# The second expert layer of a two-layer kernel, turned so that its hidden features lie on the partitions

## What is computed

```python
# x: (1024, 256), 32 experts, INTER = 96, TOP_K = 8, TAU = 0.05
logits = x @ gate_weight.T
probs = softmax(logits)
topv, topi = top_k(probs, TOP_K)
# ... thresholded by TAU and renormalised: routing_weights
combine = zeros((T, 32)).at[arange(T)[:, None], topi].add(routing_weights)

def expert_step(acc, xs):
    w_gu, w_d, c_e = xs
    gu = x @ w_gu.T
    g, u = split(gu, 2, axis=-1)
    h = silu(g) * u
    return acc + h @ w_d.T * c_e[:, None], None
out = scan(expert_step, zeros_like(x), (gate_up_proj, down_proj, combine.T))
x = _layernorm(x + out)
```

## Time and profile before

| | us |
|---|---|
| median of 3 runs | 672.63 |
| the three runs | 671.83, 672.63, 681.43 |
| span of the profiled execution (first to last instruction) | 627.6 |
| PE busy in it | 555.8 (89%) |
| DVE, ACT, POOL busy | 354.2, 237.4, 269.0 |
| mean granted clock of PE | 0.945 |

### The profile page before, as it was taken

The page is one execution under the profiler, slowest core; times in us unless marked ns, Lnnn a source line. Parts: engine busy times, 40 slices in busy tenths (PEclk is TensorE's granted clock), DMA queues, the critical chain, the costliest instruction groups (busy, mean ns, idle before and its releaser), DMA issues.

```text
span 627.6 us, 11175 instructions
## 1 busy us (share of the span) xinstructions
PE 555.8 (89%) x3453; PEld 481.3 (77%) x3453; DVE 354.2 (56%) x970; ACT 237.4 (38%) x617; POOL 269.0 (43%) x257
## 2 busy tenths in 40 slices
PE   8999985099989999989887778899999999999994
PEld 4666675078879889866444566899999999999994
DVE  4636686636664444338999566664444443444445
ACT  4645542245546665336020142233332333323234
POOL 3484024778987877602787600004042240404000
PEclk9979997589999999989998797899999999999998
DMA  8999891255876676400000420002020202000001
GB/s 259 372 387 384 284 333 52 105 177 168 232 225 188 192 237 185 133 0 1 1 1 0 152 75 2 0 1 70 8 77 2 76 0 75 0 0 0 0 0 67
DMA packets 58605, 70.93 MB, mean 113 GB/s; under 512 B 5681, under 2 KB 53570, under 8 KB 58562
## 3 DMA queue, kind: packets, MB, share of 16 engines
q10 hardware_dynamic: 35968, 35.26, 16.9%
q1 hardware_dynamic: 19234, 26.18, 13.4%
q0 software_dynamic: 3360, 8.93, 4.5%
...
## 4 chain that ended last, share of the span: by engine, by line
PE 67%; DVE 11%; DMA 5%; issue 4%; POOL 3%; ACT 3%; ACTq 1%; DVEq 0%; POOLq 0%
PE PS L1746 47%; DMA FA<-xg 5%; PE PS L2040 3%; POOL xg L662 3%; DVE FA L1700 2%; PE PS L1970 2%; DVE PS L1682 2%; PE PS L2065 2%; PE PS L2176 1%; PE PS L1821 1%; PE PS L1843 1%; PE PS L2089 1%; PE PS L2188 1%; PE PS L1983 1%; PE PS L1806 1%
## 5 line engine op out<-in xcount | busy, mean ns | idle before, releaser
L1746 PE MATMUL PS<-EW,XH 128*128 128x384 f32 (+3 forms) x764 | 215.4, 364 | 6.7 <-DVE SQ L1485 3.1
L1746 PEld LDWEIGHTS PS<-EW,XH 128*128 128x128 f32 x764 | 131.4, 193 | 11.9 <-DVE SQ L1485 3.4
L1485 DVE SCALAR_TENSOR_TENSOR SQ<-SIL,CW,PS 128x96 f32<-128x96 f32 x256 | 69.0, 311 | 116.6 <-ACT SIL L918 115.8
L1746 PE MATMUL PS<-EW,XL 128*128 128x384 f32 (+3 forms) x382 | 133.6, 350 | 0.0
L1746 PE MATMUL PS<-EW,EHH 128*128 128x256 f32 (+1 forms) x476 | 102.3, 290 | 0.2
L918 ACT ACTIVATE SIL<-PS 128x192 f32<-128x192 f32 x128 | 42.6, 332 | 158.0 <-PE PS L1746 158.0
L1746 PE MATMUL PS<-EW,EHL 128*128 128x256 f32 (+1 forms) x286 | 80.4, 281 | 0.0
L1746 PEld LDWEIGHTS PS<-EW,EHH 128*128 128x128 f32 (+1 forms) x476 | 78.5, 189 | 1.4 <-issue 0.6
L629 POOL TENSOR_TENSOR round_mark<-round_mark 128x1 f32<-128x1 f32 x10 | 1.9, 194 | 175.0 <-PE PS L1746 167.9
L1746 PEld LDWEIGHTS PS<-EW,XL 128*128 128x128 f32 x382 | 73.2, 192 | 2.1
L1746 PEld LDWEIGHTS PS<-EW,EHL 128*128 128x128 f32 (+1 forms) x286 | 54.0, 189 | 0.0
(11 more groups left out here) (373 smaller groups left out, 1048.5 us busy)
## 6 DMA issues: line engine op xcount, KB each, us to landing
...
FA<-xg ACTq DMA_DIRECT2D x47, 128.0 KB, 2.9
yg<-FA ACTq DMA_DIRECT2D x47, 128.0 KB, 3.0
...
EG<-in_gateup SPq DMA_DIRECT2D x4, 768.0 KB, 4.5
FA<-in_gateup SPq DMA_DIRECT2D x4, 768.0 KB, 4.6
```

Source lines behind the costliest of these rows:

```text
L1485: ins = dve.scalar_tensor_tensor(out=HH[:, pos % 2, h:h + W], in0=SIL[:, s, j * W:(j + 1) * W], scalar=c, in1=bank(s)[:, I + j * W:I + (j ...
L1746: ins = pe.matmul(o, l, r, start=start and i == 0, stop=stop and i == n - 1, skip_group_check=True)
```

## The change

The order of the second expert layer is turned. The gate/up weights become the stationary operand, 128 hidden features (a chunk; three chunks make a quad's 384) at a time, and 512 tokens (a half) move; so the hidden features come out on the partitions, in which form `down` takes them as its stationary operand, and no transposes are needed. There are 8 quads x 3 chunks x 2 halves = 48 steps, halves inside. A step has 12 matmuls of 512 columns (6 for gate, 6 for up, in two banks) and, 10 steps later (`LAG`), 12 of 256 columns (4 token tiles x 3).

With the features on the partitions the routing weight is no longer a scalar per partition but a row over tokens, the same for the 96 partitions of an expert. `CW` is made whole on DVE ahead of the steps, PE turns it (`turn_weights`, behind step 5), ACT and DVE copy it out, SP stores it to DRAM (`cw_room`, 128 KB) and reads it back spread over the partitions: for each pair of steps 512 KB in two DMAs (`load_spread`; one read serves both halves), in two buffers. POOL multiplies with it (`weighted`). The product silu x up is made by POOL in the first six steps (`AHEAD`, up copied by ACT) and by DVE from step 6.

The gate/up weights are loaded in four DMAs a quad, and POOL splits the quads 2 to 7 piece by piece between its steps (`next_split`). The residual moves ahead of the router. The router's products now have 128 tokens stationary and 64 columns moving (32 matmuls) and come out with tokens on the partitions; DVE adds the two halves. The last layer norm works in two halves of 4 tiles, the first waiting for all steps but the last. In place of a loop all steps are written out. Four semaphores of the first layer become one, with no change of order.

```diff
+        CHUNKS = 3
+        QUADS = E1 // QUAD
+        STEPS = QUADS * 2 * CHUNKS
+        LAG = 10
+        AHEAD = 6
+        MIXED, SPREADS, TURNED = 13, 2, 3
+        mixed = FA[:, KD * QUAD * 2 * I1:KD * QUAD * 2 * I1 + MIXED * BANK].rearrange("p (s c) -> p s c", s=MIXED)
...
+        def step_of(i):
+            return i // (2 * CHUNKS), i % 2, i // 2 % CHUNKS
+        def step_bank(i):
+            return 2 * ((i + 1) % 2 if i < AHEAD else i % 2)
+        def bank_before(i):
+            return i - 1 if i == AHEAD else i - 2
...
+            def load_spread(i):
+                n = i // 2
+                q, _, c = step_of(i)
+                if n >= SPREADS:
+                    sp.wait_ge(weighted, 2 * (n - SPREADS + 1))
...
+            sp.wait_ge(cw_step, CW_COPIED)
+            sp.dma_start(cw_room, cw_turned).then_inc(cw_stored, 16)
+            sp.wait_ge(cw_stored, 16)
+            for i in range(STEPS):
+                if i % 2 == 0:
+                    load_spread(i)
+                q = i // 6 + 4
+                if i % 6 == 2 and q < QUADS:
+                    load_gate(q)
+                q = (i - 11) // 6 + 4
+                if i >= 11 and i % 6 == 5 and q < QUADS:
+                    load_down(q)
...
+            def next_split(i):
+                at, j = divmod(i, 2 * CHUNKS)
+                q = at + 1
+                if 2 <= q < QUADS:
+                    g, gh, gl, _, _, _ = quad_slot(q)
+                    if j == 0:
+                        pool.wait_ge(gate_up_mm, 2 * 2 * CHUNKS * (q - 1))
+                        pool.wait_ge(gate_ld[q % 2], 32 * KD * (q // 2 + 1))
+                        rounded["g0"] = high(gh, g, half(0))
+                    if j == 2:
+                        low(gl, g, gh, half(0), rounded["g0"])
+                    if j == 3:
+                        rounded["g1"] = high(gh, g, half(1))
+                    if j == 4:
+                        low(gl, g, gh, half(1), rounded["g1"]).then_inc(gate_split, 1)
+                q = at - 1
+                if 2 <= q < QUADS:
+                    _, _, _, d, dh, dl = quad_slot(q)
+                    if j == 0:
+                        pool.wait_ge(dn_done, 2 * CHUNKS * (q - 1))
+                        pool.wait_ge(down_ld[q % 2], 16 * (q // 2 + 1))
+                        rounded["d"] = high(dh, d, whole)
+                    if j == 1:
+                        low(dl, d, dh, whole, rounded["d"]).then_inc(down_split, 1)
+            rounded = {}
+            for i in range(STEPS + LAG - 1):
+                if i < AHEAD:
+                    pool.wait_ge(sil_done, i + 1)
+                    pool.wait_ge(up_copied, i + 1)
+                    pool.tensor_tensor(mixed[:, i % MIXED, :], sil_t[:, i % 2, :], up_t[:, i % 2, :], ALU.mult
+                                       ).then_inc(mixed_pool, 1)
+                v = i - (LAG - 1)
+                if v >= 0:
+                    if v < AHEAD:
+                        pool.wait_ge(mixed_pool, v + 1)
+                    else:
+                        pool.wait_ge(mixed_dve, v - AHEAD + 1)
+                    n = v // 2
+                    pool.wait_ge(spread_ld[n % SPREADS], 32 * (n // SPREADS + 1))
+                    pool.tensor_tensor(mixed[:, v % MIXED, :], mixed[:, v % MIXED, :],
+                                       spread_w[n % SPREADS][:, v % 2 * BANK:(v % 2 + 1) * BANK], ALU.mult
+                                       ).then_inc(weighted, 1)
+                next_split(i)
...
+            def moe_act():
+                for i in range(STEPS + LAG - 1):
+                    if i < STEPS:
+                        b = step_bank(i)
+                        act.wait_ge(gate_up_mm, 2 * i + 1)
+                        if 2 <= i < AHEAD + 2:
+                            act.wait_ge(mixed_pool, i - 1)
+                        elif i >= 2:
+                            act.wait_ge(mixed_dve, i - 1 - AHEAD)
+                        act.activation(sil_t[:, i % 2, :], bank(b), ACT.Silu).then_inc(sil_done, 1)
+                        if i < AHEAD:
+                            act.wait_ge(gate_up_mm, 2 * i + 2)
+                            act.activation(up_t[:, i % 2, :], bank(b + 1), ACT.Copy).then_inc(up_copied, 1)
+                        if i == AHEAD - 1:
+                            act.wait_ge(cw_step, CW_TURNED)
+                            act.activation(cw_turned[:, 0:BANK], bank(2)[0:E1, :], ACT.Copy).then_inc(cw_step, 1)
+                    v = i - (LAG - 1)
+                    if v >= 0:
+                        act.wait_ge(weighted, v + 1)
+                        if v >= TURNED:
+                            act.wait_ge(dn_done, v - TURNED + 1)
+                        act.activation(h_hi[:, v % TURNED, :], mixed[:, v % MIXED, :], ACT.Copy).then_inc(h_hi_done, 1)
...
+            def combine():
+                shape = [P, NT, E1 // 2, 8]
+                each = lambda x: x.unsqueeze(2).broadcast_to(shape)
+                for e0 in (0, E1 // 2):
+                    ch.link(dve.tensor_tensor(hot, iota_e[:, e0:e0 + E1 // 2].unsqueeze(1).unsqueeze(3).broadcast_to(shape),
+                                              each(tif[:]), ALU.is_equal))
+                    ch.link(dve.tensor_tensor(hot, hot, each(t2[:]), ALU.mult))
+                    ins = dve.tensor_reduce(CW[:, :, e0:e0 + E1 // 2], hot, AX_X, ALU.add)
+                    if e0 == 0:
+                        ch.link(ins)
+                ins.then_inc(cw_step, 1)
+            def moe_dve():
+                dve.wait_ge(cw_step, CW_TURNED)
+                dve.tensor_copy(cw_turned[:, BANK:2 * BANK], bank(3)[0:E1, :]).then_inc(cw_step, 1)
+                for i in range(AHEAD, STEPS + LAG - 1):
+                    if i < STEPS:
+                        dve.wait_ge(sil_done, i + 1)
+                        dve.wait_ge(gate_up_mm, 2 * i + 2)
+                        if i >= MIXED:
+                            dve.wait_ge(h_lo_done, i - MIXED + 1)
+                        dve.tensor_tensor(mixed[:, i % MIXED, :], sil_t[:, i % 2, :], bank(step_bank(i) + 1), ALU.mult
+                                          ).then_inc(mixed_dve, 1)
+                    v = i - (LAG - 1)
+                    if v >= 0:
+                        dve.wait_ge(h_hi_done, v + 1)
+                        dve.tensor_tensor(h_lo[:, v % TURNED, :], mixed[:, v % MIXED, :], h_hi[:, v % TURNED, :].bitcast(F32),
+                                          ALU.subtract).then_inc(h_lo_done, 1)
+            def layernorm_halves(n, dst):
+                for f in range(2):
+                    tiles = slice(f * HALF, (f + 1) * HALF)
+                    dve.wait_ge(dn_done, STEPS - (1 - f))
+                    for t in range(f * HALF, (f + 1) * HALF):
+                        ins = dve.bn_stats(st[:, t, :], pair_bank(t))
+                    ch.link(ins)
...
+                    for t in range(f * HALF, f * HALF + 2):
+                        dve.tensor_scalar(dst[:, t, :], pair_bank(t), mv[:, t, 0:1], rstd[:, t:t + 1], ALU.subtract,
+                                          ALU.mult).then_inc(x_dve, 1)
...
             def router(tp, c, E):
-                for hf in range(2):
-                    pe.wait_ge(lo_done, tp * (NT // 2) + 2 * (hf + 1))
+                for t in range(NT):
+                    if t % 2 == 0:
+                        pe.wait_ge(lo_done, tp * (NT // 2) + t // 2 + 1)
                     for i in range(2 * KD):
-                        ins = pe.matmul(bank(hf)[0:2 * WRC, :], WRS[:, i // 2, :],
-                                        (XH, XL)[i % 2][:, i // 2, hf * BANK:(hf + 1) * BANK],
-                                        start=(i == 0), stop=(i == 2 * KD - 1))
-                    ins.then_inc(rt_mm, 1)
-                pe.wait_ge(lt_read, 2)
-                for t in range(NT):
-                    ins = pe.matmul(bank(2)[:, t * E:(t + 1) * E], LT[:, t * P:(t + 1) * P],
-                                    wr_sum[0:2 * WRC, c:c + E], start=(t == 0), stop=True, skip_group_check=True)
+                        k = i // 2
+                        both = WRS[:, k, :].rearrange("p (s e) -> p s e", s=2)[:, :, c:c + E]
+                        ins = pe.matmul(bank(0)[:, t * 2 * E:(t + 1) * 2 * E].rearrange("p (s e) -> p s e", s=2),
+                                        (XH, XL)[i % 2][:, k, t * P:(t + 1) * P], both,
+                                        start=(t == 0 and i == 0), stop=(i == 2 * KD - 1), skip_group_check=True)
                 ins.then_inc(rt_mm, 1)
...
+            def chunk_of(w, k, up, c):
+                first = (k * 2 + up) * CHUNKS * P + c * P
+                return w[:, first:first + P]
+            def moe_pe():
+                def gate_up(i):
+                    q, hf, c = step_of(i)
+                    b = step_bank(i)
+                    if i % (2 * CHUNKS) == 0:
+                        pe.wait_ge(gate_split, q + 1)
+                    before = bank_before(i)
```

(46 more changed lines are left out.)

376 lines of the change are left out of this document (148 added, 228 removed).

## The result

| | before | after |
|---|---|---|
| median of 4 runs each, us | 672.23 | 648.24 |
| lowest and highest, us | 669.88, 681.43 | 647.19, 657.47 |
| ratio, 95% interval | | 0.9634 (0.9598 to 0.967) |
| matmuls | 3453 | 3085 |
| busy, us: PE | 555.8 | 544.1 |

What follows compares the result with a forecast made beforehand. PE's own matmul stream was taken as the bound. Start -4.0, first step to last matmul -27.5 and end +1.2 gave -30.3 us: span 597.3, with 45.0 around it 642.3 us, range 636 to 654.

Steps and rivals of the forecast that it cites:

- time with the 45.0 around it: Whole execution: 45.0 us taken to lie around the forecast span of 597.3 us, giving 642.3 us.
- Start: Second layer, token turning, residual and router: first step 4.0 us earlier, at 384.8 instead of 388.78 us.
- Steps: PE's 48 steps: 4.19 us each from 0.2319 and 0.1175 us per matmul, 201.3 us against 224.1 before.
- Rival C: PE's matmul columns come at the full 2.4 GHz in long rows: 17.0 us less, 625.3 us; 3 in 100.
- The wait for `CW`: PE, after steps 0 to 5, waits 0.5 us for DVE's combine weights before turning them.
- ready at R + 17.2: DVE's combine weights finished 17.2 us after R, the first step's start; `combine` itself 7.5 us with waits.
- rival A: Later start: slower `combine`, reduce, clock drop and late first spread read, together some +6, 648.3 us; 15 in 100.
- Middle as a whole: First step to last matmul: 201.3 + 0.5 + 0.9 = 202.7 us against 230.2, so -27.5.
- Steady steps at no cost: POOL's weighting and splitting, 61% busy, and DVE, ACT and SP work stay hidden behind PE: cost 0.
- End: Last layer norm in halves: 6.0 us after the last matmul, 1.2 more than before, bounds 0 to +2.
- Sum: Whole kernel: -4.0 before the first step, -27.5 to the last matmul, +1.2 after it, together -30.3 us.
- Rival B: Spread reads, in series with POOL, become the bound beyond 8.0 us a read; 688 us at 11.3; 5 in 100.

Runs made afterwards that it cites:

- changed_again: The changed kernel, unedited, run again beside the kernel before on the same chip: 606.94 us, ratio 0.9621 to the kernel before.
- whole_norm: The changed kernel with its last layer norm in one piece again instead of halves: 608.44 us, ratio 0.9603 to the kernel before.

## Why the prediction was right, and where it was off

**Base.** The step "time with the 45.0 around it" is wrong: 1.8 us lie around a span. It did no harm, because the sum was a difference put on the median, and the 43 us are spent by both kernels. Had the time been forecast as span and surroundings of the execution shown, at 597.3 + 1.8, it would have been 49 us off the first comparison, and 8 off changed_again.

**Start** (forecast -4.0): -5.0. The router's 32 matmuls are 0.111 us apart, 3.7 us in all (forecast 0.1 and 3.2). The residual ended 6.75 us behind the start of the turning where 8.2 were forecast: the clock was low for some 3 us (0.50 from 417.4 to 420.4), not for the 5.7 assumed. This hangs on when the clock rises, which moved the first step between 9.11 and 11.44 us in the runs above, so the 1 us of agreement is not worth much.

**Steps** (201.3): 48 x 4.22 = 202.6. The interval at 512 columns is 0.233 us (0.2319 by the earlier trace rows) and at 256 columns 0.12, not 0.1175. Rival C is out: long rows of one size came no quicker.

**The wait for `CW`** is the step that failed. "`combine` whole is six operations over 1024 elements, 1.22 us each" and "ready at R + 17.2": two of the six took 2.2 us and three small ones ahead of them 0.9 to 1.3 in place of some 0.2, beside POOL's first products. The prediction saw the contention in POOL's own rows, 1277 and 1827 ns, and costed it where it is harmless, in the steady steps. It is paid where DVE is the critical engine and POOL has just been given work. With the clock this is 4.0 + 1.8 us; rival A had it in kind, with 1.7 us for DVE where 4.6 came, 1.5 for the clock where 1.8 came, and 2 us for a late read that didn't come. By the prediction's own mark, a wait of over 3 us, it is A that happened. The time lies in the range because the range was drawn to take A in. That it meets A's 648.3 to the tenth is luck: A's terms were off, and losses that it didn't have (2.6 us in the steps and the last `down`, below) were made up for by 1.8 us less at the start and the end.

**Middle as a whole.** From the first step to the last matmul 211.2 us in place of 202.7: +4.0 the wait, +1.8 turn and clock behind it, +1.4 the last eleven `down` (16.9 us where 15.5 were forecast, 0.4 of it a wait for DVE), +1.2 the 37 steps of 4.22, rest 0.1. Against the 230.2 of before it is -19.0.

**Steady steps at no cost**: right. POOL is 60% busy (a weighting took 1.45 us on the mean, between the 1.28 and the 1.83 of the prediction), PE waits for nothing in 37 steps, the first `down` didn't wait for its weights.

**End** (+1.2): 9.04 us from the last matmul against 8.59, +0.45; whole_norm shows that the halves are no part of it.

**Sum**: -5.0 - 19.0 + 0.4 = -23.6 us, measured -24.0, forecast -30.3.

**Rival B**: its mechanism is real, with its wait where it was put. Its threshold is nearer than it had: an estimated 6.7 us in place of 8.0, and the slowest read of the changed kernel was complete 6.3 us behind its first issue.
